# Tail of an attention and SwiGLU kernel in rounds of four products and four output steps

## The chip, the cores and the metric

The kernel runs on one core of a Trainium2 chip. The metric is the device time of one execution in microseconds (us). Before the change the median of three runs was 777.21 us (777.11, 777.21 and 779.03).

## The reference, cut to what matters

Eight batches of 512 tokens with 256 channels pass one transformer block and a conditioned layer norm, all in 32-bit floats:

```python
x = x + a_alpha * attention(ada_rmsnorm(x, t, attn_gamma_w, attn_beta_w), W_q, W_k, W_v, W_o)   # 16 heads of 16
h = ada_rmsnorm(x, t, ffn_gamma_w, ffn_beta_w)
x = x + f_alpha * (silu(h @ gate_w.T) * (h @ hidden_w.T) @ out_w.T + out_b)                     # hidden width 1024
out = (layernorm(x) * weight + bias + tanh(t @ lin_w.T + lin_b)) * weight + bias
```

`gamma`, `beta` and `alpha` are one row per batch, made from the 64 numbers of `t`. Every projection is made as a sum of three products of high and low parts, so one 256-wide contraction of a tile takes six matmuls or, in tiles of 64 rows, twelve.

## The kernel before, in words

Each engine has its own instruction stream, written by a Python function `unit(n)` that is called for n = 0, 1, 2, ... up to `LAST` = 164. Semaphores tie the streams together. There are 16 units per batch. For n below `NU` = 128 a unit does one 128-key block of attention for one group of four heads. From n = `GH_AT` = 28 on, each unit also has one **product** of the feed-forward part, number e = n - 28, from 0 to 127.

- **Product e** (`gate_hidden`, L1323): 24 matmuls in tiles of 64 rows, two side by side, for hidden columns 128 (e mod 8) and on, of half batch e // 8 (256 tokens). The gate and the value land in two banks of PSUM. Then ScalarE takes the tanh (L861), VectorE makes the silu and multiplies (L1070, L1077, `act_y`), ScalarE rounds to the high part (L868, `a_hi`), and the low part `a_lo` is made by GpSimd (L554) while attention runs, by VectorE (L1083) in the tail. `a_hi` and `a_lo` are rings of six.
- **Output step e** (`project_out`, L1336): 6 matmuls with the full 128 rows that add product e's share to the output of the half. It waits for `a_lo` of e.
- **Jobs** are other pieces of TensorE work given to units by a table. In the tail four are left, all of the last batch (7): `WO` 0 and 1 (projection of the attention output, L1210, units 134 and 135), `FT` 0 and `FT` 1 (transposes of the normalised half, L1248, units 137 and 141), which make the inputs of products 112 to 119 and 120 to 127.

The **tail** begins at n = 128, where the scores of the last attention block are done. TensorE has products 100 to 127, output steps 96 to 127, the last `attend` (L1296) and the four jobs left. `tail_units` writes them in rounds. Three pairs of banks (`ps_m`, `ps_x`, `ps_s`) take the products in turn, so product e waits for `act_y` of product e - 3. All output steps of a half add up in the bank `ps_o`; when eight are done VectorE multiplies the sum by `f_alpha` (`scale(("H", half))`, L1042), GpSimd adds it to x (`add_to_x`, L579), VectorE takes mean and variance (`statistics`, L1062) and GpSimd normalises (`moments`, `normalise`, `weigh`). The first output step of the next half waits for that multiplication.

Before `WO` 0 of batch 7 can run, the output of the last attention group goes a long way: ScalarE copies it out of PSUM (L845), it is written to memory, the sums of the softmax are read back, inverted, written and broadcast (`out_scratch`, `d_s`, `reciprocal_scratch`, `d_c`), GpSimd multiplies (L562), ScalarE rounds (L854) and GpSimd makes the low part (L567, `on_lo`). Before product 112 can run, `WO` 0 is scaled and added to x, squared on ScalarE (L742), the root taken on GpSimd (L510, L512), normalised (L771), transposed (`FT` 0), split in high and low parts (L825, L996, L1004), and a DMA swaps the two halves of the rows (`n_x`, L378); the second half of the product's matmuls reads `n_x`. The same goes for `FT` 1 and product 120.

The order of each stream is the order in which the functions are called; a wait on one instruction holds all that is behind it on that engine.

Of the kernel before, what the change touches and what calls it, by code (L numbers as in the profile page):

```python
# [12 lines left out]
B = 8  # L13
# [10 lines left out]
JC = HID // P  # L24
# [3 lines left out]
UNITS = NG * TT  # L28
NU = B * UNITS
# [6 lines left out]
GH_AT = 28  # L36
# [35 lines left out]
def chunk_at(n):  # L72
# [3 lines left out]


SC = sorted([(CHUNK_AT + CH * c, 0, ("F", c)) for c in range(CHUNKS)]
            + [(GH_AT + LAG + JC * (hf + 1), 0, ("H", hf)) for hf in range(CHUNKS * CH // JC, 2 * B)]
            + [(n, 1, job_at(n)) for n in range(LAST) if job_at(n) and job_at(n)[0] == "WO"])  # L80
SC_NO = {what: no + 1 for no, (_, _, what) in enumerate(SC)}

# [6 lines left out]
def build(nc, dram):  # L89
    with ExitStack() as ctx:  # L90
# [401 lines left out]
        def _(pool):  # L492
# [76 lines left out]
            def add_to_x(what):  # L569

                hf = {"F": what[1] * CH // JC, "H": what[1]}.get(what[0])
                b, h = (what[2], what[1]) if what[0] == "WO" else (hf // 2, hf % 2)
                pool.wait_ge(sc_r, SC_NO[what])
                if what[0] == "WO":
                    pool.wait_ge(xr_in[h][b % 2], 16 * (b // 2 + 1))
                else:
                    pool.wait_ge(bias_r, 2 * b + h + 1)
                xs = xr[:, b % 2, 2 * h:2 * h + 2]
                pool.tensor_tensor(xs, xs, sc[:], ALU.add).then_inc(x_add, 1)  # L579
# [77 lines left out]
            def unit(n):  # L657
                b, u = n // UNITS, n % UNITS
                e = n - GH_AT - 1

                def at(k, d):
                    return u == k and 0 <= b + d < B

                if at(0, 1):
                    n_low(b + 1, 0)
                if at(1, 1):
                    n_low(b + 1, 1)
                if job_at(n - 1) and job_at(n - 1)[:2] == ("FT", 1) and n < NU:
                    n2_low(job_at(n - 1)[2], 1)
                if at(4, -1):  # L670
                    o_norm(b - 1, 1)
                if at(10, -1) and n < NU:
                    n2_low(b - 1, 0)
                if at(11, -2):
                    moments(b - 2, 0)
                    normalise(b - 2, 0)
                if at(10, 2):
                    root1(b + 2)
                if at(12, -1) and n < NU:
                    norm2(b - 1, 1)  # L680
                if at(13, 0):
                    o_norm(b, 0)
                if chunk_at(n - 1) is not None:
                    add_to_x(("F", chunk_at(n - 1)))
                if 0 <= e < TAIL:
                    a_low(e)
                if n in PIECE_AT:
                    split_piece(PIECE_AT.index(n))
                if at(1, -3) and b - 3 < B - 1:
                    moments(b - 3, 1)  # L690
                    normalise(b - 3, 1)
                    weigh(b - 3, 1)
                if at(1, 0) and b > 0:
                    v_copy(b, 3)
                if at(5, -1):
                    o_low(b - 1, 1)
                if at(6, -2) and n >= NU:
                    add_to_x(("H", 2 * (b - 2)))
                if at(7, -1) and n < NU:
                    add_to_x(("WO", 0, b - 1))  # L700
                if at(8, -1) and n < NU:
                    norm2(b - 1, 0)
                    add_to_x(("WO", 1, b - 1))
                if n == NU + 7:
                    root2(B - 1, 0)
                if n == NU + 9:
                    root2(B - 1, 1)
                if at(9, -1):
                    add_bias(b - 1, 0)
                if at(11, -2):  # L710
                    weigh(b - 2, 0)
                if at(13, -1):
                    add_bias(b - 1, 1)
                if at(14, 1):
                    for g in range(NG - 1):
                        v_copy(b + 1, g)
                if at(14, 0):
                    o_low(b, 0)
                if at(14, -2) and NU <= n < LAST - JC:
                    add_to_x(("H", 2 * (b - 2) + 1))  # L720

            for n in range(LAST):
                unit(n)
# [248 lines left out]
        def _(dve):  # L972
# [59 lines left out]
            def scale(what):  # L1032

                no = SC_NO[what]
                if no > 1:
                    dve.wait_ge(x_add, no - 1)
                if what[0] in "FH":
                    step = {"F": CH, "H": JC}[what[0]]
                    end = step * (what[1] + 1)
                    dve.wait_ge(f_done, end)  # L1040
                    dve.wait_ge(tab_f_in, 16 * ((end - 1) // (2 * JC) + 1))
                    dve.tensor_tensor(sc[:], ps_c if what[0] == "F" else ps_f, tab_f[:].unsqueeze(1).broadcast_to([P, 2, D]),  # L1042
                                      ALU.mult).then_inc(sc_r, 1)
                else:
                    dve.wait_ge(job_full, JOB_NO[what])
                    dve.wait_ge(tab_a_in, 16 * (what[2] + 1))
                    dve.tensor_tensor(sc[:], ps_j[:].rearrange("p (t n) -> p t n", t=2),
                                      tab_a[:, 0:1, :].broadcast_to([P, 2, D]), ALU.mult).then_inc(sc_r, 1)
# [37 lines left out]
            def last_norm():  # L1086

                hf = 2 * B - 1
                dve.wait_ge(sc_r, SC_NO["H", hf])
                dve.wait_ge(bias_r, hf + 1)  # L1090
                xs = xr[:, hf // 2 % 2, 2:4]
                dve.tensor_tensor(xs, xs, sc[:], ALU.add).then_inc(x_add, 1)
                statistics(B - 1, 1)
                dve.wait_ge(mv_r, 2 * (hf + 1))
                for t in range(2):
                    dve.scalar_tensor_tensor(out=xs[:, t], in0=xs[:, t], scalar=mv[:, t, 0:1], in1=w2[:],
                                             op0=ALU.subtract, op1=ALU.mult).then_inc(z_last_r, 1)
                dve.wait_ge(rstd3_r, hf + 1)
                for t in range(2):
                    dve.wait_ge(z_last_r, t + 1)  # L1100
                    dve.scalar_tensor_tensor(out=xs[:, t], in0=xs[:, t], scalar=rstd3[:, t:t + 1], in1=tab_b[:],
                                             op0=ALU.mult, op1=ALU.add).then_inc(z_last_r, 1)
# [39 lines left out]
            def unit(n):  # L1142
                b, u = n // UNITS, n % UNITS
                e = n - GH_AT

                def at(k, d):
                    return u == k and 0 <= b + d < B

                if n == 0:
                    evac(("TR", 0, 1), n)  # L1150
                if n + LEAD < NU:
                    reduce_max(2 * (n + LEAD))
                if n + LEAD < NU:
                    reduce_max(2 * (n + LEAD) + 1)
                if at(6, -2) and n >= NU:
                    scale(("H", 2 * (b - 2)))
                if at(14, -2) and n >= NU:
                    scale(("H", 2 * (b - 2) + 1))
                if 0 <= e < TAIL:
                    gate(e)  # L1160
                if at(10, -2):
                    statistics(b - 2, 0)
                if at(0, -3) and b - 3 < B - 1:
                    statistics(b - 3, 1)
                if chunk_at(n) is not None:
                    scale(("F", chunk_at(n)))
                if job_at(n) and n < NU:
                    evac(job_at(n), n)
                if at(2, -1):
                    o_recip(b - 1, 1)  # L1170
                if at(11, 0):
                    o_recip(b, 0)
                if TAIL <= e - 1 < NE:
                    a_low(e - 1)
                if TAIL <= e < NE:
                    gate(e)
                if job_at(n) and n >= NU:
                    evac(job_at(n), n)
# [6 lines left out]
        def _(pe):  # L1185
# [267 lines left out]

            def tail_units(n):
                e = n - GH_AT
                for d in range(2):
                    if e + d < NE:
                        gate_hidden(e + d)
                if n == NU:
                    attend(n - 1)  # L1460
                job(n)
                for d in range(CHUNKS * CH if n == NU else e - 2, e):
                    if d < NE:
                        project_tail(d)
                job(n + 1)

            for n in range(GH_AT):
                early_unit(n)
            for n in range(GH_AT, NU):
                middle_unit(n)  # L1470
            for n in range(NU, LAST, 2):
                tail_units(n)

# [27 lines left out]
```

## Time and profile before

| | |
|---|---|
| median of three runs | 777.21 us |
| the profiled execution, its own time | 781.7 us |
| its span, first to last instruction | 779.9 us |
| mean granted clock of TensorE | 0.976 of full |
| busy: TensorE, VectorE, ScalarE, GpSimd | 721.0, 536.2, 470.8, 392.1 us |

The busy share of TensorE is 92% of the span, and in most of the 40 slices of the page it is 90% or more. The tail lies in the last four slices, from about 694 us on. The granted clock is 1.00 in most stretches and lower in a few: 1.00 stands for 2.4 GHz, 0.50 for 1.2 GHz. Matmuls are pipelined, so a matmul that lasts 0.28 us can be followed by the next one 0.12 us after its start; what a piece of work costs is read from the distance of starts, or from the chain of waits.

### The profile page before, as it was taken

How to read it: one execution, taken by the hardware profiler on the slowest of the kernel's cores; microseconds unless marked ns; L12 is line 12 of the kernel's file. 1: busy time of each engine (PE TensorE's matmuls, PEld its weight loads, DVE VectorE, ACT ScalarE, POOL GpSimd, SP SyncE). 2: the span in 40 equal slices, each digit the busy share in tenths (PEclk: the TensorE clock that was granted, in tenths of full speed). 3: DMA queues.
4: the chain of work that ended last, by engine and by line, in shares of the span. 5: the costliest groups of instructions: out<-in, count | busy, mean ns of one | idle time of the engine just before them, and what ended most of it. 6: DMA issues, size and time to landing. Idle time of an engine off the chain costs nothing.

```text
span 779.9 us, 17477 instructions
## 1 busy us (share of the span) xinstructions
PE 721.0 (92%) x6646; PEld 489.3 (63%) x6646; DVE 536.2 (69%) x795; ACT 470.8 (60%) x858; POOL 392.1 (50%) x493
## 2 busy tenths in 40 slices
PE   5678787899999999999999999999999999999995
PEld 4333233455676767675676667776677667679895
DVE  3576675678667776777667776768667776536765
ACT  4347574778566756667666756667666655753431
POOL 4335331345248553666348553766447453872433
PEclk9769998999999999999999999999999999999998
DMA  6855655445442644445442553445443440242110
GB/s 193 270 176 182 203 189 166 163 124 210 132 165 68 202 144 148 140 137 183 132 164 80 192 162 131 137 137 158 137 157 102 172 141 15 58 116 64 49 50 28
DMA packets 63676, 108.75 MB, mean 139 GB/s; under 512 B 10240, under 2 KB 17848, under 8 KB 63592
## 3 DMA queue, kind: packets, MB, share of 16 engines
q1 hardware_dynamic: 62760, 106.78, 43.0%
q8 instruction: 53, 0.87, 0.5%
q10 hardware_dynamic: 704, 0.66, 0.3%
q0 software_dynamic: 128, 0.20, 0.1%
q14 instruction: 31, 0.25, 0.1%
HBM read 59.60 MB, written 39.09 MB: 127 GB/s over the span
## 4 chain that ended last, share of the span: by engine, by line
PE 69%; DVE 9%; DMA 8%; issue 6%; ACT 4%; SPq 3%; POOL 1%; ACTq 0%; POOLq 0%; DVEq 0%
PE ps_x L1323 16%; PE ps_j L1210 11%; PE ps_o L1296 11%; PE ps_j L1336 9%; PE ps_s L1283 9%; PE ps_m L1270 6%; DVE mx L1030 4%; DMA out_scratch<-o_raw 2%; PE ps_o L1336 2%; ACT prob L837 2%; DVE fx L996 2%; DMA qs<-m_hl 1%; DVE gate_t L1070 1%; PE ps_m L1323 1%; DMA prob<-in_wk 1%
## 5 line engine op out<-in xcount | busy, mean ns | idle before, releaser
L1030 DVE TENSOR_REDUCE mx<-ps_m 128x2 f32<-128x1024 f32 x222 | 271.6, 1223 | 126.4 <-PE ps_m L1270 125.9
L837 ACT ACTIVATE prob<-ps_s 128x1024 f32<-128x1024 f32 x256 | 262.0, 1024 | 82.4 <-PE ps_s L1283 81.8
L1283 PE MATMUL ps_s<-qs,ks 64*128 64x512 f32 x512 | 120.4, 466 | 21.5 <-ACT prob L837 15.0
L1296 PE MATMUL ps_o<-prob,v 128*32 128x512 f32 x1024 | 139.0, 615 | 0.2 <-ACT o_raw L845 0.2
L1283 PEld LDWEIGHTS ps_s<-qs,ks 64*128 64x128 f32 x512 | 48.7, 186 | 141.0 <-issue 73.8
L1270 PE MATMUL ps_m<-ks,qs 64*128 64x512 f32 x444 | 94.0, 419 | 9.3 <-DVE mx L1030 5.6
L1323 PE MATMUL ps_x<-n,gh_hi 64*128 64x256 f32 x872 | 97.8, 284 | 1.6 <-DVE act_y L1077 1.6
L554 POOL TENSOR_TENSOR a_lo<-act_y,a_hi 128x256 fp32r<-128x256 f32 x100 | 73.7, 737 | 46.5 <-ACT a_hi L868 46.3
L1323 PE MATMUL ps_x<-n_x,gh_hi 64*128 64x256 f32 x872 | 94.3, 276 | 0.0
L579 POOL TENSOR_TENSOR xr<-xr,sc 128x512 f32<-128x512 f32 x41 | 53.3, 1300 | 63.1 <-DVE sc L1042 40.6
L1323 PEld LDWEIGHTS ps_x<-n,gh_hi 64*128 64x128 f32 x872 | 74.3, 184 | 13.6 <-DVE act_y L1077 10.1
L1323 PEld LDWEIGHTS ps_x<-n_x,gh_hi 64*128 64x128 f32 x872 | 74.4, 185 | 0.0
L868 ACT ACTIVATE a_hi<-act_y 128x256 fp32r<-128x256 f32 x128 | 52.7, 412 | 27.2 <-DVE act_y L1077 27.2
L562 POOL TENSOR_TENSOR d_c<-on_lo,d_c 128x512 f32<-128x512 f32 x16 | 20.6, 1287 | 92.0 <-DMA d_c<-reciprocal_scratch 92.0
L861 ACT ACTIVATE gate_t<-ps_x 128x256 f32<-128x256 f32 x109 | 41.8, 383 | 34.6 <-PE ps_x L1323 34.1
L1323 PE MATMUL ps_x<-n,gh_lo 64*128 64x256 f32 x436 | 61.1, 276 | 0.0
L1323 PE MATMUL ps_x<-n_x,gh_lo 64*128 64x256 f32 x436 | 61.1, 276 | 0.0
L1336 PE MATMUL ps_j<-ow_hi,a_hi 128*128 128x256 f32 x192 | 56.5, 294 | 0.0
L1270 PEld LDWEIGHTS ps_m<-ks,qs 64*128 64x128 f32 x444 | 43.1, 190 | 20.1 <-DVE mx L1030 15.6
L1070 DVE SCALAR_TENSOR_TENSOR gate_t<-gate_t,ps_x 128x256 f32<-128x256 f32 x109 | 44.8, 411 | 13.8 <-ACT gate_t L861 13.8
L1336 PE MATMUL ps_j<-ow_hi,a_lo 128*128 128x256 f32 x192 | 54.0, 281 | 0.0
L1336 PE MATMUL ps_j<-ow_lo,a_hi 128*128 128x256 f32 x192 | 54.0, 281 | 0.0
(176 smaller groups left out, 1439.6 us busy)
## 6 DMA issues: line engine op xcount, KB each, us to landing
qs<-stack_scratch SPq DMA_DIRECT2D x31, 512.0 KB, 5.1
ks<-stack_scratch SPq DMA_DIRECT2D x31, 512.0 KB, 6.4
stack_scratch<-qk_hi SPq DMA_DIRECT2D x56, 256.0 KB, 3.2
out_scratch<-o_raw SPq DMA_DIRECT2D x32, 256.0 KB, 2.9
n_x<-n SPq DMA_DIRECT2D x32, 256.0 KB, 3.7
stack_scratch<-qk_lo SPq DMA_DIRECT2D x28, 256.0 KB, 3.5
on_lo<-out_scratch SPq DMA_DIRECT2D x16, 256.0 KB
d_c<-reciprocal_scratch SPq DMA_DIRECT2D x16, 256.0 KB
```

The lines of the kernel that those rows point to most:

```text
L554: pool.tensor_tensor(a_lo[:, e % RING, :], act_y[:, e % 2, :], a_hi[:, e % RING, :].bitcast(F32), ALU.subtract)\
L579: pool.tensor_tensor(xs, xs, sc[:], ALU.add).then_inc(x_add, 1)
L837: act.activation(prob[:, n % 2, 2 * h:2 * h + 2, :], ps_s[:], ACT.Exp, scale=SCALE).then_inc(p_r, 1)
L868: act.activation(a_hi[:, e % RING, :], act_y[:, e % 2, :], ACT.Copy).then_inc(a_hi_r, 1)
L1030: dve.tensor_reduce(mx[:, group % 2, :, h, qt], max_pair(mp)[:], AX.X, ALU.max).then_inc(mx_red, 1)
L1070: dve.scalar_tensor_tensor(out=gate_t[:], in0=gate_t[:], scalar=1.0, in1=g_part(e), op0=ALU.add, op1=ALU.mult).then_inc(s_r, 1)
L1210: mm = pe.matmul(out, lhs(a, k), rhs(c, k), start=(n == 0), stop=(n == len(steps) - 1))
L1270: mm = pe.matmul(max_pair(mp)[:, s, :], qs[r:r + 64, g, j, qt * P:(qt + 1) * P], ks[r:r + 64, g, j, :], start=True, stop=True)
L1283: mm = pe.matmul(ps_s[:, s, :], ks[r:r + 64, g, j, kb * P:(kb + 1) * P], qs[r:r + 64, g, j, :], start=True, stop=True)
L1296: mm = pe.matmul(ps_o[32 * i:32 * i + 32, :], v[:, g, kb, i, :], prob[:, n % 2, i, :], start=(kb == 0), stop=(kb == TT - 1), skip_group_ch ...
L1323: mm = pe.matmul(bank[:, r, 0:HT], GH[a][rows, 2 * k + (r ^ x), j * P:(j + 1) * P], N2[x][rows, h, c, k, :], start=(m == 0), stop=(m == 11))
L1336: mm = pe.matmul(out[:, t, :], A[a][:, e % RING, t * P:(t + 1) * P], OW[c][:, j, :], start=(first and m == 0 and t == 0), stop=(end and m ...
```

## The change

`tail_units` writes four products, then up to three jobs, then four output steps, then a fourth job, where it wrote two products, a job, two output steps and a job. The last `attend` keeps its place behind product 101. The other streams keep one unit per product. Because a half's last output step now stands at another place in TensorE's stream, the units at which VectorE and GpSimd take up the sum of a half are moved: for halves 12 to 14 from n = 134, 142 and 150 to n = 136, 144 and 152, which puts the sum of half 12 behind `WO` 0 and `WO` 1. Statistics and normalisation of half 13 go two units later (n = 144 to 146, 145 to 147). The scaling of half 15 moves from the stream's unit 158 into `last_norm`.

```diff
-            + [(GH_AT + LAG + JC * (hf + 1), 0, ("H", hf)) for hf in range(CHUNKS * CH // JC, 2 * B)]
+            + [(NU + (GH_AT + JC * (hf + 1) - NU + 3) // 4 * 4 + 4, 0, ("H", hf)) for hf in range(CHUNKS * CH // JC, 2 * B)]
 # GpSimd
-                if at(1, -3) and b - 3 < B - 1:
+                if at(1 if n < NU + UNITS else 3, -3) and b - 3 < B - 1:
                     moments(b - 3, 1)
-                if at(6, -2) and n >= NU:
+                if at(8, -2) and n >= NU:
                     add_to_x(("H", 2 * (b - 2)))
-                if at(14, -2) and NU <= n < LAST - JC:
-                    add_to_x(("H", 2 * (b - 2) + 1))
+                if at(0, -3) and NU < n < LAST - JC:
+                    add_to_x(("H", 2 * (b - 3) + 1))
 # VectorE
             def last_norm():
                 hf = 2 * B - 1
+                scale(("H", hf))
-                if at(6, -2) and n >= NU:
+                if at(8, -2) and n >= NU:
                     scale(("H", 2 * (b - 2)))
-                if at(14, -2) and n >= NU:
-                    scale(("H", 2 * (b - 2) + 1))
+                if at(0, -3) and NU < n < LAST - JC:
+                    scale(("H", 2 * (b - 3) + 1))
-                if at(0, -3) and b - 3 < B - 1:
+                if at(0 if n < NU + UNITS else 2, -3) and b - 3 < B - 1:
                     statistics(b - 3, 1)
 # TensorE
             def tail_units(n):
                 e = n - GH_AT
-                for d in range(2):
+                for d in range(4):
                     if e + d < NE:
                         gate_hidden(e + d)
-                if n == NU:
-                    attend(n - 1)
-                job(n)
-                for d in range(CHUNKS * CH if n == NU else e - 2, e):
+                    if n + d == NU + 1:
+                        attend(NU - 1)
+                for d in range(3):
+                    job(n + d)
+                for d in range(e - 4, e):
                     if d < NE:
                         project_tail(d)
-                job(n + 1)
+                job(n + 3)
-            for n in range(NU, LAST, 2):
+            for n in range(NU, LAST, 4):
                 tail_units(n)
```

The order that this gives on TensorE in the whole tail, in short (P product, O output step, A the last attend):

```
before: P100 P101 A O96-99 | P102 P103 O100 O101 | P104 P105 O102 O103 | P106 P107 WO0 O104 O105 WO1 |
        P108 P109 O106 O107 FT0 | P110 P111 O108 O109 | P112 P113 O110 O111 FT1 | ... | P126 P127 O124 O125 | O126 O127
after:  P100 P101 A P102 P103 O96-99 | P104-107 WO0 O100-103 WO1 | P108-111 FT0 O104-107 |
        P112-115 FT1 O108-111 | P116-119 O112-115 | P120-123 O116-119 | P124-127 O120-123 | O124-127
```

TensorE at the last attend (first row), before the change:

```order
L1296 MATMUL ps_o<-prob,v 32x512 x4
L1336 MATMUL ps_o<-ow_hi,a_hi 128x256
L1336 MATMUL ps_o<-ow_hi,a_lo 128x256
L1336 MATMUL ps_o<-ow_lo,a_hi 128x256
L1336 MATMUL ps_o<-ow_hi,a_hi 128x256
```

and with it:

```order
L1297 MATMUL ps_o<-prob,v 32x512 x4
L1324 MATMUL ps_s<-n,gh_hi 128x256 x2
L1324 MATMUL ps_s<-n,gh_lo 128x256 x2
L1324 MATMUL ps_s<-n,gh_hi 128x256 x4
L1324 MATMUL ps_s<-n,gh_lo 128x256 x2
```

Product 102 now stands where output step 96 stood; the four output steps follow behind product 103.

TensorE at `FT` 0 of batch 7 (the row with `fx`), before:

```order
L1336 MATMUL ps_o<-ow_hi,a_hi 128x256
L1336 MATMUL ps_o<-ow_hi,a_lo 128x256
L1336 MATMUL ps_o<-ow_lo,a_hi 128x256
L1248 MATMUL ps_j<-ident,fx 128x128 x4
L1323 MATMUL ps_x<-n,gh_hi 128x256 x2
L1323 MATMUL ps_x<-n,gh_lo 128x256 x2
```

and with the change:

```order
L1324 MATMUL ps_s<-n_x,gh_lo 128x256 x2
L1324 MATMUL ps_s<-n_x,gh_hi 128x256 x2
L1249 MATMUL ps_j<-ident,fx 128x128 x4
L1337 MATMUL ps_o<-ow_hi,a_hi 128x256
L1337 MATMUL ps_o<-ow_hi,a_lo 128x256
L1337 MATMUL ps_o<-ow_lo,a_hi 128x256
```

`FT` 0 stood between output step 107 and product 110; it now stands between product 111 and output step 104.

VectorE around the two `WO` jobs (L1047, L1013) and the sum of half 12 (L1042), where the rows with a minus are of before and those with a plus of after:

```order
+L1047 TENSOR_TENSOR sc<-ps_j,tab_a 128x512
+L1013 TENSOR_TENSOR xr<-xr,sc 128x512
 L1042 TENSOR_TENSOR sc<-ps_o,tab_f 128x512
 L1083 TENSOR_TENSOR a_lo<-act_y,a_hi 128x256
-L1070 SCALAR_TENSOR_TENSOR gate_t<-gate_t,ps_m 128x256
-L1077 TENSOR_TENSOR act_y<-ps_m,gate_t 128x256
-L1047 TENSOR_TENSOR sc<-ps_j,tab_a 128x512
-L1013 TENSOR_TENSOR xr<-xr,sc 128x512
```

The sum of half 12 is taken up behind both `WO` jobs and no longer ahead of them. No stream has an instruction more or less than before; those of ScalarE and of the DMA queue keep their order.

## Rows read from the trace of the kernel before

**Rows 1.** Waits of TensorE in the tail, 694.4 to 772 us.

```profile
PE ps_o L1336 <- DVE a_lo L1083: 2.5, 2, 1.5
PE ps_j L1210 <- POOL on_lo L567: 0.7, 1, 0.7
PE ps_o L1336 <- ACT o_raw L845: 0.7, 1, 0.7
PE ps_m L1323 <- DMA n_x<-n: 0.4, 1, 0.4
PE ps_o L1336 <- DVE sc L1042: 0.4, 1, 0.4
```

**Rows 2.** Chain of waits, last attend to WO 0: start us, us, what.

```profile
697.57 1.04 PE ps_o L1296 x8
...
699.25 2.03 DMA out_scratch<-o_raw
...
708.10 3.64 DMA d_c<-reciprocal_scratch
...
713.90 1.29 POOL on_lo L567
...
715.33 1.67 PE ps_j L1210 x12
```

**Rows 3.** Chain of waits: output steps in pairs (x12), products one by one (x24).

```profile
717.00 1.42 PE ps_o L1336 x12
...
744.62 1.61 PE ps_o L1336 x12
746.23 1.60 PE ps_m L1323 x24
747.83 1.40 PE ps_x L1323 x24
```

**Rows 4.** Timeline of VectorE: start us, us, line, tiles; silu part of product 100.

```profile
699.99 0.42 DVE L1077 TENSOR_TENSOR act_y<-ps_m,gate_t 128x256 f32<-128x256 f32 x1
```

**Rows 5.** Chain of waits, FT 0 to the second half of product 112.

```profile
724.45 0.45 PE ps_j L1248 x4
...
728.54 3.52 DMA n_x<-n
...
732.11 0.97 PE ps_m L1323 x12
```

**Rows 6.** Timeline at the end of the tail; brackets: idle before, and releaser.

```profile
769.86 1.26 POOL L638 TENSOR_TENSOR xr<-xr,tab_b 128x512 f32<-128x512 f32 x1
769.90 1.50 DVE L1083 TENSOR_TENSOR a_lo<-act_y,a_hi 128x256 fp32r<-128x256 f32 x1 [0.48 <-ACT a_hi L868]
```

**Rows 7.** Chain of waits, the last output step.

```profile
771.46 0.99 PE ps_o L1336 x6
```

**Rows 8.** Timeline of TensorE: gaps by waits on a DMA.

```profile
28.79 0.79 PE L1270 MATMUL ps_m<-ks,qs 64*128 64x512 f32 x2 [2.21 <-DMA ks<-stack_scratch]
...
93.71 0.79 PE L1283 MATMUL ps_s<-qs,ks 64*128 64x512 f32 x2 [2.96 <-DMA qs<-m_hl]
...
128.03 0.80 PE L1283 MATMUL ps_s<-qs,ks 64*128 64x512 f32 x2 [3.11 <-DMA qs<-m_hl]
```

**Rows 9.** TensorE by microsecond: stretch, its length, busy, PEclk, DMA share, GB/s.

```profile
93.00:94.00 1.00, 0.29 (x2) 0.64 0.13 22
...
96.00:97.00 1.00, 1.00 (x6) 0.65 0.93 236
...
127.00:128.00 1.00, 0.00 (x0) 0.71 0.10 22
...
134.00:135.00 1.00, 1.00 (x8) 0.88 0.87 338
```

**Rows 10.** Timeline of TensorE at half clock: first and sixth of six equal matmuls.

```profile
132.79 0.41 PE L1210 MATMUL ps_j<-w_lo,n_hi 128*128 128x256 f32 x1
...
133.85 0.41 PE L1210 MATMUL ps_j<-w_hi,n_lo 128*128 128x256 f32 x1
```

## The prediction, made before the changed kernel ran

> **What bounds the kernel now.** First I read the page: TensorE is busy for 92% of the span, so what the change is worth depends on whether TensorE in the tail still has something to do at every moment. Next the waits of TensorE between 694.4 and 772 us [rows 1]: four kinds, together 4.7 us of idle time, the largest 1.5 us just ahead of the last output step. So the tail is bound by TensorE's own work, with a few short waits. Then the chain of waits, for two stretches that TensorE does not set: the way of the attention output into `WO` 0 [rows 2], and the way of `FT` 0 into product 112 [rows 5]. Last the clock by microseconds, where TensorE waited long [rows 8, 9].
>
> **Prices.** A product costs 1.40 us behind another product and 1.60 behind a tile of another shape; two output steps cost 1.42 us behind work in full tiles and 1.61 behind a product [rows 3]. Each change of shape thus costs 0.20 us, a single output step 0.71 us. The six low-clock matmuls of the same size stand 1.06 / 5 = 0.212 us apart [rows 10]; at full clock it is 1.42 / 12 = 0.118 us [rows 3]. So a microsecond of TensorE work done at half clock loses 1 - 0.118 / 0.212 = 0.44 us.
>
> **What is removed.** From 28 changes of shape in the tail 15 are left (there are half as many rounds, but product 102 now stands behind attend). 13 x 0.20 = 2.6 us less. The wait of output step 96 for `o_raw` (0.7) goes, since products 102 and 103 stand in front of it. The wait at the end (1.5) goes too: there the last `a_lo` lasted 1.50 us, beside a GpSimd pass of 1.26 us [rows 6], and only three output steps stood between product 127 and the last step; now seven do, 5 us, and `a_lo` of 127 is due some 4 us behind product 127. I give `a_lo` the same 1.5 us; without that cover the 1.5 us would be back.
>
> **What is added, first gap.** `WO` 0 starts at 715.33 [rows 2], 16.7 us behind the end of attend at 698.61, after three transfers and two GpSimd passes. None of these waits for TensorE, and attend keeps its place, so `WO` 0 cannot start sooner with the change. What TensorE has ahead of it shrinks by output steps 100 to 103. By hand: product 102 from 698.5 to 700.1; product 103 takes the banks of product 100 and waits for its `act_y`, over at 699.99 + 0.42 = 700.41 [rows 4], so it runs from 700.5 to 701.9; steps 96 to 99 take 1.61 + 1.42, to 704.9; products 104 to 107 take 1.60 + 3 x 1.40 = 5.8, to 710.8. Their banks are free in time: tanh, silu, high part and low part of a product are some 2.2 us together, and one product starts every 1.4 us with three pairs of banks. From 710.8 to 715.3 TensorE has nothing: **4.5 us of idle time**, where 0.7 stood.
>
> **Second gap.** From 715.33: `WO` 0 1.67, steps 100 to 103 2.84, `WO` 1 1.42, products 108 to 111 1.60 + 4.20, and `FT` 0 begins at 727.06 on the chain's reckoning, 0.2 later still as its shape differs from the product in front of it. Before it stood at 724.45, and from there to the second half of product 112 the chain took 732.11 - 724.45 = 7.66 us, of which 3.52 is the swap `n_x` [rows 5]. That way is ScalarE, VectorE and DMA, all unchanged, so `n_x` is there at 727.26 + 7.66 = 734.9. ScalarE has the normalised half ready about 724, so `FT` 0 waits for nothing but its turn. The cover behind `FT` 0 is itself, 0.65, steps 104 to 107, 2.84, and the first half of product 112, 0.90: to 731.45. **Idle for 3.5 us**, where 0.4 stood. Before, two products and two steps (4.4 us) lay there. On GpSimd `root2` of the first half now stands ahead of the sum of half 12, a pass of 1.3 us, but ScalarE's squares do not come earlier (they stand behind tanh 107, which waits for step 100), so I cost that at nothing.
>
> **The rest.** From 734.9: second half of product 112 0.97, products 113 to 115 4.20, `FT` 1 0.65, steps 108 to 111 2.84; twice four products and four steps, 5.80 + 3.03 each; then products 124 to 127 5.80 and eight steps 1.61 + 4.26. Together 38.0 us, plus 0.3 for a wait of product 119 for `act_y` of 116, which is held up by the statistics of half 13. That ends at 773.2; before it ended at 771.46 + 0.99 = 772.45 [rows 7]. Behind it VectorE scales and normalises half 15 as before. So at full clock the change costs **+0.8 us**: the idle time added takes all that the shapes and the short waits give back. The sums of halves 13 and 14, their statistics and normalisation end 10 us or so before somebody needs them; two units later they are hidden by products.
>
> **The clock.** Every gap of TensorE of 2.2 us or more in the middle of its work was followed by half clock: 2.21, 2.96 and 3.11 us [rows 8]. From the clock means, the second one fell at 93.28 (0.64 is 0.28 at full and 0.72 at half) and rose at 96.70, which is 3.0 us of work at 1.2 GHz behind the gap's end at 93.71; the third fell at 127.42 and rose at 134.24, 6.2 us behind 128.03 [rows 9]. Both new gaps, 4.5 and 3.5 us, are longer than these. So a fall costs 3.0 x 0.44 = 1.3 to 6.2 x 0.44 = 2.7 us; the two rows are equally near, I take 4.6 us and 2.0 us for each gap. All of it is on the path, as behind both gaps TensorE has work without a wait. The Trainium skill ("TensorE: Matmul & The Clock Gate", "Why this matters for your kernels") says that long idle gaps between bursts of matmuls bring the half clock back; by that rule, which speaks against this change, the loss is there as in the rows; without it the sum would stay at +0.8.
>
> **Sum.** +0.8 + 2 x 2.0 = +4.8 us. The profiled execution took 781.7 us (span 779.9) against a median of 777.2; the difference does not touch a change in the tail, so I add to the median: **782.0 us**. Bounds of the unknown: both falls at the low row +3.4 (780.6), both at the high row +6.2 (783.4).
>
> The 0.20 us per change of shape has a rival price on the page "TensorE: Matmul & The Clock Gate" of the Trainium skill ("LDWEIGHTS"): 128 columns at 1.2 GHz, 0.107 us, if just one weight load were laid bare; 13 changes would then give an estimate of 1.4 us instead of 2.6, and the sum would be 1.2 us higher. The trace's own 0.20 decides.
>
> **Rivals.**
> - *One fall only.* The second gap is broken by half a product, and the clock may stay up, or the second fall may overlap less work. +0.8 + 1.3 to 2.7: 779.3 to 780.7. Against it: 2.21 us sufficed once.
> - *No fall.* 778.0, no change that can be told. For it: I have three gaps only, all in attention, none among work in full tiles.
> - *Faster.* The attention output reaches `WO` 0 sooner than it did: three transfers lie in that chain, and `out_scratch` took 2.03 us where the page's median to landing is 2.9, so they vary. If they took 3 us less, the old order could have gained 0.7 of it and the new one gains all: 2.3 better than +0.8, the first gap shrinks to 1.5 us and does not lower the clock. With the second gap's clock kept as well: 777.2 + 0.8 - 2.3 = 775.7. It decides once the chain is shorter by 1.5 us or more. Against it: this transfer was quick already.
> - *Worse.* Transfers longer by 1 us each widen both gaps: +3 on the high row, 785.
>
> **How the numbers follow.** Chances: both falls 0.62, one fall 0.18, none 0.09, faster 0.05, worse 0.06. A measurement of this kernel tells a change from none at about 0.3%, 2.3 us. Slower by more: 0.62 + 0.06 + 0.11 of the one-fall case = 0.79; within: 0.09 + 0.07 = 0.16; faster 0.05. The range runs from 778.6, which leaves out no fall and the faster case, to 784.0.
>
> **What would show it.** In the new trace: `WO` 0 at the same distance from attend, with 4 to 5 us of idle time on TensorE ahead of it; product 112 waiting 3 to 4 us for `n_x`; granted clock of 0.50 behind both; no wait ahead of the last output step; 1.61 us for the first pair of steps of a round and 1.42 for the second. The forecast is wrong if the clock stays at 1.00 behind the gaps, or if `WO` 0 starts well before 16.7 us behind attend.

## The result and the profile after

With the change the kernel takes 782.81 us (median of seven runs, 779.23 to 784.36) against 779.03 us before (seven runs, 776.51 to 780.95, the first three included); the ratio is 1.0048 with a 95% interval of 1.0027 to 1.0069, which is 3.7 us, 2.1 to 5.4. It is slower, by half a percent. The profiled execution has a span of 782.5 us.

A whole run varies by some us with what happens in its first 170 us: attend ends at 698.61 us in the trace of before and at 695.92 in the trace of after, though both run the same instructions up to there. (In all twelve traces the attention part from about 170 to about 690 us takes the same time to 0.3 us.) So below the traces are compared by two stretches of the chain of waits: the **tail**, from the end of the last attend to the end of the last output step, and the **late tail**, from the start of `WO` 0 to the same end. The tail took 73.84 us before [rows 2, 7] and 775.08 - 695.92 = 79.16 after; the late tail 57.12 and 62.16.

The waits of TensorE in the tail of after (us in total, times, longest), which answer to [rows 1]:

```profile
PE ps_j L1211 <- POOL on_lo L567: 4.6, 1, 4.6
PE ps_m L1324 <- DMA n_x<-n: 3.3, 1, 3.3
PE ps_m L1324 <- DVE act_y L1077: 0.3, 1, 0.3
```

The six short waits of before have become two long ones and one short one. `o_raw`, the sum of half 13 and the two `a_lo` no longer hold anything up; `on_lo` and `n_x` hold up six and eight times as much.

The chain of waits of after, answering to [rows 2, 3, 5, 7] (start us, us, what):

```profile
694.88 1.04 PE ps_o L1297 x8
...
712.92 2.90 PE ps_j L1211 x12
715.82 3.09 PE ps_o L1337 x24
...
726.12 0.60 PE ps_j L1249 x4
...
730.36 3.52 DMA n_x<-n
...
733.93 1.65 PE ps_m L1324 x12
735.58 2.56 PE ps_x L1324 x24
738.14 2.37 PE ps_s L1324 x24
...
760.37 3.03 PE ps_o L1337 x24
...
769.20 5.88 PE ps_o L1337 x48
```

`WO` 0 starts 17.0 us behind attend (16.7 before). Its twelve matmuls take 2.90 us, not 1.67, and the products behind `n_x` take 2.56 and 2.37 us, not 1.40: that is half clock. Four output steps cost 3.03 us, one change of shape for four; the last eight run through without a wait. The granted clock by microseconds (stretch, length, busy, PEclk, DMA share, GB/s), answering to [rows 9]:

```profile
712.00:713.00 1.00, 0.08 (x1) 0.93 0.00 0
713.00:714.00 1.00, 1.00 (x5) 0.50 0.08 16
...
716.00:717.00 1.00, 1.00 (x10) 0.87 0.00 0
...
733.00:734.00 1.00, 0.07 (x2) 0.67 0.01 4
...
740.00:741.00 1.00, 1.00 (x20) 0.92 0.00 0
```

From 712.86 to 716.26 and from 733.34 to 740.16 TensorE had 1.2 GHz: 3.3 and 6.2 us of work behind the ends of the gaps at 712.92 and 733.93.

### The profile page after: what moved, and what is told of

Same layout as the page of the kernel before. It is cut to its first block, busy times and chain, and to the rows that moved or that the text cites. A ratio compares the mean times of both kernels' runs of the same rounds, so it can differ in the third digit from the quotient of the medians.

```text
span 782.5 us, 17477 instructions
## 1 busy us (share of the span) xinstructions
PE 720.2 (92%) x6646; PEld 491.3 (63%) x6646; DVE 535.3 (68%) x795; ACT 469.6 (60%) x858; POOL 391.8 (50%) x493
## 4 chain that ended last, share of the span: by engine, by line
PE 68%; DMA 10%; DVE 9%; issue 5%; ACT 4%; SPq 3%; POOL 1%; ACTq 0%; POOLq 0%; DVEq 0%
PE ps_x L1324 16%; PE ps_j L1211 11%; PE ps_o L1297 11%; PE ps_j L1337 9%; PE ps_s L1284 8%; PE ps_m L1271 6%; DVE mx L1030 3%; DMA out_scratch<-o_raw 3%; PE ps_o L1337 2%; ACT prob L837 2%; DMA qs<-m_hl 2%; DVE fx L996 2%; PE ps_m L1324 1%; PE ps_s L1324 1%; DVE gate_t L1070 1%
## 5 line engine op out<-in xcount | busy, mean ns | idle before, releaser
L1284 PEld LDWEIGHTS ps_s<-qs,ks 64*128 64x128 f32 x512 | 48.5, 185 | 140.5 <-issue 71.3
L1324 PEld LDWEIGHTS ps_x<-n,gh_hi 64*128 64x128 f32 x872 | 74.9, 186 | 13.3 <-DVE act_y L1077 10.0
L1070 DVE SCALAR_TENSOR_TENSOR gate_t<-gate_t,ps_x 128x256 f32<-128x256 f32 x109 | 44.8, 411 | 11.8 <-ACT gate_t L861 11.7
```

The source lines that it names most:

```text
L1070: dve.scalar_tensor_tensor(out=gate_t[:], in0=gate_t[:], scalar=1.0, in1=g_part(e), op0=ALU.add, op1=ALU.mult).then_inc(s_r, 1)
L1284: mm = pe.matmul(ps_s[:, s, :], ks[r:r + 64, g, j, kb * P:(kb + 1) * P], qs[r:r + 64, g, j, :], start=True, stop=True)
L1324: mm = pe.matmul(bank[:, r, 0:HT], GH[a][rows, 2 * k + (r ^ x), j * P:(j + 1) * P], N2[x][rows, h, c, k, :], start=(m == 0), stop=(m == 11))
```

## The experiments

The granted clock and the chain of each kernel come from one trace per kernel; the ratios come from 7 to 12 timed runs of each (e5, e8 and e10 have the profiled run alone). Each kernel's late tail is read from its trace by the same two rows of the chain, the start of `WO` 0 and the last output steps:

| kernel | WO 0 starts | last step ends | late tail | against before | ratio to before (95%) |
|---|---|---|---|---|---|
| before | 715.33 | 772.45 | 57.12 | | |
| the change | 712.92 | 775.08 | 62.16 | +5.04 | 1.0048 (1.0027 to 1.0069) |
| e1 both gaps filled | 713.07 | 770.99 | 57.92 | +0.80 | 1.0002 (0.9983 to 1.0021) |
| e5 first gap filled | 709.77 | 769.23 | 59.46 | +2.34 | one run |
| e8 second gap filled | 717.04 | 776.40 | 59.36 | +2.24 | one run |
| e10 first gap in part, second filled | 711.72 | 769.58 | 57.86 | +0.74 | one run |
| e2 FT 0 sooner | 715.69 | 772.58 | 56.89 | -0.23 | 1.0008 (0.9987 to 1.0029) |
| e6 steps 100 to 103 ahead of WO 0 | 711.42 | 769.16 | 57.74 | +0.62 | 1.0022 (1.0003 to 1.0041) |
| e3 fours from unit 144 on | 709.04 | 763.24 | 54.20 | -2.92 | 0.9967 (0.9941 to 0.9993) |
| e4 fours from unit 136, FT 0 sooner | 714.25 | 767.87 | 53.62 | -3.50 | 0.9953 (0.9931 to 0.9975) |
| e7 as e4, step 108 sooner | 710.07 | 763.71 | 53.64 | -3.48 | 0.9944 (0.9923 to 0.9964) |
| e9 as e7, FT 1 sooner | 717.74 | 770.65 | 52.91 | -4.21 | 0.9918 (0.9892 to 0.9944) |

### e1: both gaps filled

```diff
+            def keep_busy(count):
+                job_evacuated(last[0])
+                for _ in range(count):
+                    pe.matmul(ps_j[:, 0:D], ow_hi[:, 0, 0:P], ow_lo[:, 0, :], start=True, stop=True)
 # in gate_hidden
+                if e == 112:
+                    keep_busy(24)
 # in job, ahead of run
+                    if job_at(n) == ("WO", 0, B - 1):
+                        keep_busy(34)
```

Expected:

> The changed kernel with matmuls whose result nobody reads in both gaps of TensorE: 34 ahead of WO 0 (34 x 0.118 = 4.0 of the 4.6 us) and 24 ahead of product 112 (2.8 of the 3.3 us). My theory (gaps set by chains that do not touch TensorE, plus half clock behind each): WO 0 and n_x come no sooner, the granted clock stays at 1.00 behind both, and the 9.5 us of work at 1.2 GHz give back 9.5 x 0.44 = 4.2 us; ratio to before 1.001 (+0.8 to +1.1 us). Rival, that the clock is not the cause and the rounds of four cost by themselves: ratio stays at 1.005.

Waits of TensorE in this kernel:

```profile
PE ps_j L1211 <- POOL on_lo L567: 0.6, 1, 0.6
PE ps_m L1332 <- DMA n_x<-n: 0.4, 1, 0.4
```

and its chain at both ends of the late tail:

```profile
713.07 1.69 PE ps_j L1211 x12
714.76 2.84 PE ps_o L1345 x24
...
765.11 5.88 PE ps_o L1345 x48
```

`WO` 0 came 17.3 us behind attend, no sooner than in the others, so the filling took nothing away from the chain; its matmuls took 1.69 us and the steps behind it 2.84, full clock. The clock stayed at 1.00 from attend to the last output step. The late tail is 0.80 us longer than before, the full-clock term of the prediction; 4.2 us of the 5.0 belong to the clock. The time agrees (1.0002, interval 0.9983 to 1.0021).

### e5, e8 and e10: one gap at a time, and a short gap

The same edit with `keep_busy(34)` alone (e5), `keep_busy(24)` alone (e8), and with 22 and 24 (e10).

Expected of e5:

> The changed kernel with only the first gap filled (34 matmuls whose result nobody reads, ahead of WO 0). Measured by the tail, from the end of the last attend to the end of the last output step: 73.84 us before, 79.16 with the change, 75.18 with both gaps filled. My theory, each gap with its own stretch at half clock: the granted clock stays at 1.00 behind WO 0 and still falls behind the wait for n_x, which stays 3.3 us; the tail is shorter by the 3.3 us at 1.2 GHz x 0.44 = 1.5 us: 77.7 us (plus or minus 0.5 for the transfers). Rival, one fall brings the other: the second stretch goes too and the tail is 75 us.

Expected of e8:

> The changed kernel with only the second gap filled (24 matmuls whose result nobody reads, ahead of product 112). My theory: the clock falls behind the first gap and stays at 1.00 behind the second; the stretch of 6.2 us at 1.2 GHz, 2.7 us, is given back: tail 79.2 - 2.7 = 76.5 us; the first stretch may last 3.0 to 6.2 us, which makes it 76.3 to 77.8. Rival, that the long stretch behind the second gap comes from the shape of the work there and not from the idle time: the clock falls all the same and the tail stays at 79 us.

Expected of e10:

> The changed kernel with 22 matmuls whose result nobody reads ahead of WO 0 (2.6 of the 4.6 us, so that 2.0 us of idle time are left) and 24 ahead of product 112. Gaps of 1.7 us so far left the clock up, one of 2.2 us and all longer ones were followed by half clock. If the length of the gap decides between these, 2.0 us is open: with no fall the stretch from WO 0 to the end of the last step is 57.9 us as with both gaps filled, with a fall of 3.3 us at 1.2 GHz 59.4 us.

In e5 the clock stayed up behind `WO` 0 and fell behind `n_x`; in e8 the other way round, behind a wait of 4.7 us. So neither fall brings the other (one trace of each). The tail of e5 is 769.23 - 692.73 = 76.5 us, less than the 77.7 expected, since the second stretch at 1.2 GHz was shorter here. Waits and granted clock of e5:

```profile
PE ps_m L1330 <- DMA n_x<-n: 3.3, 1, 3.3
PE ps_j L1211 <- POOL on_lo L567: 0.4, 1, 0.4
```

```profile
729.00:730.00 1.00, 0.69 (x10) 1.00 0.00 0
730.00:731.00 1.00, 1.00 (x18) 0.68 0.08 16
...
733.00:734.00 1.00, 1.00 (x14) 0.62 0.66 260
```

The clock was down from 730.36 to 733.76, 3.4 us.

e8 has a tail of 776.40 - 700.03 = 76.4 us (76.5 expected); its stretch behind `WO` 0 also lasted 3.4 us. The same 3.3 us gap thus cost 2.7 us in the trace of after and 1.5 in e5: what varies from run to run is the length of the stretch.

In e10 the wait for `on_lo` was 1.6 us by the trace and the clock stayed at 1.00 all through the tail; the late tail is that of e1. 2.0 us had been expected to remain, so the length that was to be tried was not reached: `WO` 0 came 16.7 us behind attend here and 17.0 in the trace of after, and the 22 matmuls pushed the gap's start back by 2.8 us and not 2.6.

In the tails of the twelve traces, then, the six gaps of 3.3 us or more were each followed by a fall, those up to 1.7 us (e4, e6, e7, e10) by none, and up to the last output step no fall came without such a gap. The attention part of the same traces shows that length alone does not decide, and that the expectation's "all longer ones" goes too far. The first pair of rows is from the trace of after, the second from e10, the third again from after (for each the timeline of TensorE, then the clock):

```profile
93.00 0.51 PE L1284 MATMUL ps_s<-qs,ks 64*128 64x512 f32 x2 [3.05 <-DMA qs<-m_hl]
93.00:94.00 1.00, 1.00 (x8) 1.00 0.00 0
```

```profile
124.03 0.50 PE L1284 MATMUL ps_s<-qs,ks 64*128 64x512 f32 x2 [1.75 <-DMA qs<-m_hl]
...
125.00:126.00 1.00, 1.00 (x8) 0.50 0.23 27
```

```profile
139.02 0.50 PE L1284 MATMUL ps_s<-qs,ks 64*128 64x512 f32 x2 [0.67 <-ACT prob L837]
139.00:140.00 1.00, 0.98 (x8) 0.71 0.34 121
```

A gap of 3.05 us left the clock at 1.00, one of 1.75 us was followed by a fall, and about 139.4 us the clock fell with no gap over 0.9 us in the 5 us before. From gaps between 1.75 and 3.05 us both outcomes are on record. What else decides is not shown.

### e2: FT 0 two products sooner

```diff
                 for d in range(4):
                     if e + d < NE:
                         gate_hidden(e + d)
 # two lines left out: the last attend
+                    if job_at(n + d) == ("FT", 0, B - 1):
+                        job(n + d)
                 for d in range(3):
-                    job(n + d)
+                    if job_at(n + d) != ("FT", 0, B - 1):
+                        job(n + d)
```

Expected:

> The changed kernel with FT 0 of batch 7 behind product 109 instead of behind product 111; all else equal. My theory: FT 0 starts 2.8 us sooner, products 110 and 111 come to lie beside the way to n_x, the wait of product 112 falls from 3.3 to 0.5 us or less and the second stretch at half clock (6.2 us, 2.7 us lost) goes; two more changes of shape cost 0.4: about 5.5 us less than the changed kernel, ratio to before 0.999 to 1.000. Rival, that ScalarE's normalised half is not ready by then: FT 0 waits instead, the gap moves ahead of product 110 and the time stays near ratio 1.004.

```profile
PE ps_j L1211 <- POOL on_lo L567: 4.7, 1, 4.7
PE ps_m L1324 <- DMA n_x<-n: 0.6, 1, 0.6
```

The late tail fell by 5.3 us against the change (5.5 expected). `FT` 0 did not wait, the wait for `n_x` went from 3.3 to 0.6 us and the second stretch at half clock is gone; the first is still there. The way of `n_x` itself was no shorter, so the second gap is a matter of how much work TensorE has between `FT` 0 and product 112. The time agrees within its interval (1.0008, 0.9987 to 1.0029).

### e6: output steps 100 to 103 ahead of WO 0

```diff
                 for d in range(3):
-                    job(n + d)
+                    if n + d != NU + 6:
+                        job(n + d)
                 for d in range(e - 4, e):
                     if d < NE:
                         project_tail(d)
+                if n + 2 == NU + 6:
+                    job(n + 2)
                 job(n + 3)
```

Expected:

> The changed kernel with output steps 100 to 103 ahead of WO 0, which is followed at once by WO 1. My theory: the first gap falls from 4.6 to 1.7 us, too short for a fall of the clock (1.5 back); WO 1 now waits some 0.9 us for the scaling of WO 0; together WO 1 ends 1.9 us sooner; the second gap and its fall stay: tail 79.2 - 1.9 - 1.5 = 75.8 us, ratio to before 1.002. Rival, that the first gap is not what holds the tail but the way from WO 0 to FT 0: the second gap grows by what the first loses, tail 77.5 us or more.

```profile
PE ps_m L1324 <- DMA n_x<-n: 3.4, 1, 3.4
PE ps_j L1211 <- POOL on_lo L567: 1.7, 1, 1.7
PE ps_j L1211 <- DVE sc L1047: 0.8, 1, 0.8
```

The three waits are nearly as expected (1.7, 0.8 for 0.9, and an unchanged second gap), the clock stayed up behind the gap of 1.7 us, and the ratio is as expected too (1.0022 for 1.002). The tail is 769.16 - 694.30 = 74.9 us, 0.9 less than 75.8: again a second stretch of 3.4 and not 6.2 us. The rival, by which the second gap would grow, is out.

### e3 and e4: where rounds of four pay

e3 starts from the kernel before and gives `tail_units` a size, 2 for n up to 142 and 4 from 144 on, takes the output steps up where the round before left off, and moves the sum of half 14 alone to unit 152. Of the edit, the calls alone:

```diff
-            for n in range(NU, LAST, 2):
-                tail_units(n)
+            for n in range(NU, NU + 16, 2):
+                tail_units(n, 2)
+            for n in range(NU + 16, LAST, 4):
+                tail_units(n, 4)
```

Expected:

> Rounds of two as before up to unit 142, rounds of four from unit 144 on (products 116 to 127); the sum of half 14 two units later. My theory: neither gap opens; six changes of shape fewer (1.2 us) and no wait ahead of the last output step (1.5 us), 0.3 us lost to one wait for act_y: 2.4 us faster than before, ratio 0.997. Rival, that a change of shape costs nothing and only shows in the records: ratio 0.998 by the last wait alone; rival, that rounds of four stall on the banks: 1.000 or more.

```profile
741.12 1.61 PE ps_o L1336 x12
...
748.53 3.03 PE ps_o L1336 x24
757.36 5.88 PE ps_o L1336 x48
```

The last eight output steps run without a wait; the waits for `on_lo`, `n_x`, the first `a_lo` and the sum of half 13 are there as before. The late tail is 2.92 us shorter, half a microsecond more than expected (the wait for `act_y` that was to cost 0.3 did not come), and the ratio is 0.9967: faster, by a third of a percent. The last wait alone would give 1.5 us, so the changes of shape have their price; the interval of the time (0.9941 to 0.9993) cannot tell 0.998 from 0.997, the late tail from end to end can.

e4 has the two sizes meet at unit 136 and `FT` 0 behind product 109 as in e2.

Expected:

> Rounds of two up to unit 134 (so WO 0 and WO 1 stand as before), rounds of four from unit 136 with FT 0 behind product 109; sum of half 12 at unit 134, of 13 and 14 as in the changed kernel. My theory: WO 0 waits 0.7 us as before, n_x is there about 730.6 on the clock of the first trace and product 112 waits 1.5 us for it, too short for a fall of the clock; then 38.0 us of work: 3 to 3.6 us faster than before, ratio 0.9955 to 0.996. Rival, that a wait of 1.5 us already lowers the clock: 0.998 to 1.000.

```profile
PE ps_m L1324 <- DMA n_x<-n: 1.7, 1, 1.7
PE ps_j L1211 <- POOL on_lo L567: 0.2, 1, 0.2
```

3.50 us shorter, ratio 0.9953. The wait for `n_x` is 1.7 us for 1.5 expected, and the clock stayed up behind it.

### e7: one output step into the wait for n_x, a miss

```diff
-                for d in range(next_step[0], min(e, NE)):
+                end = 109 if n == NU + 8 else min(e, NE)
+                for d in range(next_step[0], end):
                     project_tail(d)
-                next_step[0] = e
+                next_step[0] = end
```

Expected:

> The mixed kernel with output step 108 (and 106, 107) ahead of product 112. Its step stood behind product 115. My theory: the 1.7 us wait of product 112 for n_x is filled by one step, 0.71 us, all else stays: tail 69.78 - 0.7 = 69.1 us, ratio to before 0.9945. Rival, that a_lo of 108 is late on VectorE, behind FT 0's work there: the step waits, product 112 starts later than n_x lands, and the tail stays at 69.8 or grows.

```profile
PE ps_j L1211 <- POOL on_lo L567: 1.6, 1, 1.6
PE ps_m L1324 <- DMA n_x<-n: 1.0, 1, 1.0
PE ps_s L1324 <- DVE act_y L1077: 0.2, 1, 0.2
```

The step did fill 0.7 us of the wait, and the late tail stayed at 53.64 us. (The ratio came out as 0.9944 for 0.9945 expected, but its interval and that of e4 overlap, so it does not tell the two kernels apart. The tail as a whole is 71.3 us, since `WO` 0 came 17.6 us behind attend here and 16.2 in e4: the transfers.) Not `a_lo`, the rival, took it back, but the work of `FT` 1. From the chain of e7:

```profile
730.56 0.60 PE ps_j L1249 x4
...
732.24 0.99 DVE fx L996 x2
...
734.61 0.44 DVE act_y L1077
...
735.09 1.66 PE ps_s L1324 x24
736.78 1.69 PE ps_m L1324 x24
738.50 1.68 PE ps_x L1324 x24
```

and from the chain of e4:

```profile
734.74 0.60 PE ps_j L1249 x4
...
742.67 1.67 PE ps_x L1324 x24
```

ScalarE and VectorE have `FT` 1's parts to make behind product 113, and TensorE reaches `FT` 1 behind product 115; VectorE comes to the silu of product 114 only then. The rows at 735.09, 736.78 and 738.50 are products 117, 118 and 119: each waits for the `act_y` of the product three before, and they start 1.7 us apart where 1.40 is the price. The list of waits shows only 0.2 us of this, since it counts from the modelled end of a matmul. From `FT` 1 to product 119 both kernels take 7.9 us (730.56 to 738.50 and 734.74 to 742.67): in e4 TensorE's own work just filled that way, and what the step took out of the wait for `n_x` was waited off here.

### e9: FT 1 sooner as well

```diff
             def early(n):
-                return job_at(n) == ("FT", 0, B - 1)
+                return job_at(n) in (("FT", 0, B - 1), ("FT", 1, B - 1))
```

Expected:

> The kernel of e7 with FT 1 of batch 7 behind product 113 instead of behind product 115. From the start of WO 0 to the end of the last output step e7 took 53.64 us and the mixed kernel 53.62, though its wait for n_x was 0.7 us shorter. My theory of that: ScalarE and VectorE come to FT 1's work behind product 113 and stand still until TensorE reaches it behind product 115, so act_y of product 113 is late and product 116 waits for its banks; what the step saved was waited off there. With FT 1 sooner that wait (0.7 us or more) goes and two changes of shape (0.4) come in: 53.0 to 53.3 us, ratio to before 0.994. Rival, that output steps 108 to 111 are themselves held up (by a_lo): the stretch stays at 53.6 or grows by 0.4.

```profile
717.74 1.66 PE ps_j L1211 x12
...
764.77 5.88 PE ps_o L1337 x48
```

52.91 us, 0.73 less than e7, though it has two changes of shape more: the wait for `act_y` is gone from the trace. (The products that waited in e7 were 117 to 119, behind the silu of 114 to 116, and not 116 as the expectation has it; the cause that it names, VectorE and ScalarE standing still until `FT` 1, is what the trace shows.) This is the shortest late tail of all, 4.2 us under before. Of 780 us that would be a ratio of 0.9946; the timed 0.9918 is lower, with an interval (0.9892 to 0.9944) that just leaves 0.9946 out; why it is lower is not shown.

## Why the prediction was right, point by point

- **The time.** 782.0 us forecast, 782.8 measured; but the median of before rose by 1.8 us with more runs, so that the two agree to 0.8 us is in part luck and the difference is what counts: +4.8 us forecast, +3.7 (2.1 to 5.4) measured, +5.3 in the tail of the profiled execution.
- **The waits of before.** The rows hold five kinds, six waits, and not four kinds; the sum of 4.7 us is right.
- **First gap.** 4.5 us of idle time forecast, 4.6 found; `WO` 0 at 16.7 us behind attend forecast, 17.0 found, and 16.2 to 17.6 over all the traces, whatever TensorE did in front of it (e1, e5 and e10 filled the gap and e6 put other work there). The way holds four transfers (`out_scratch`, `d_s`, `reciprocal_scratch`, `d_c`), not three; nothing in the sum hangs on their number.
- **Second gap.** 3.5 forecast, 3.3 found. e2 shows the cause.
- **Full-clock term.** +0.8 forecast; e1 has +0.80 in the late tail, where the tail alone would say +1.3, as the chain to `WO` 0 was half a microsecond longer in that run. Its parts agree too: `WO` 0 to `FT` 0 11.7 us (11.9 forecast), `FT` 0 to the second half of product 112 7.8 (7.7), from there to the end 38.4 (38.3).
- **The 0.3 us of product 119.** It was found, but the statistics of half 13 do not cause it: they come after. The chain of e1 and of after leads from `FT` 1 over VectorE's work for it and the sum of half 13 to product 119, 7.9 us, as in e4 and e7.
- **What was removed.** Last wait, `o_raw` wait and cheaper rounds are all there: 3.03 us for four output steps where twice 1.61 stood. e3 shows the last wait and the shapes together in time.
- **The clock, a term somewhat too large.** Two falls, as forecast. I took 4.6 us of work at half clock for each, from two rows of 3.0 and 6.2. The trace of after has just these, 3.3 and 6.2. But in e2, e5, e6 and e8 each stretch at 1.2 GHz lasted 3.4 us, five of the six in all, so the usual loss is 1.5 us per gap: 0.8 + 2 x 1.5 = 3.8 us. The 3.7 of the timed runs fits this, but their interval, 2.1 to 5.4, holds the 4.8 as well.
- **The falls, right with some luck.** "Every gap of 2.2 us or more" was three gaps of one trace. The trace of after has a gap of 3.05 us in attention with no fall, e3 one of 2.2 us. That both new gaps lowered the clock fits the forecast and its 0.62; that gaps of this length always do was never shown, though all six in the tails did.
- **The rivals.** "One fall only" and "no fall" did not happen in the profiled execution of the change; e2 and e6 each had one long gap left, and one fall. "Faster" asked for a chain to `WO` 0 shorter by 1.5 us or more; none of the traces had that. "Worse" has a slip in its sum: +3 on the high row would be 786.4, not 785. The rival price of a change of shape, 1.4 us for all 13, is refuted in its size by the 3.03 and 1.61 us rows: 3.03 - 4 x 0.71 is 0.19. Its mechanism is not: a weight load of an output step lasts 0.19 us in the trace of before, so one load laid bare would cost just that. No run tells whether it is the load.

Not settled: what besides its length decides whether a gap is followed by half clock, why a stretch at half clock is at times twice as long, and what share of the timed runs has it.

## What to carry to other kernels

Fewer switches between kinds of work are worth what the rows say (here 0.2 us each), but the work that is moved was also the cover of something: before regrouping, write down for every outside chain (transfers, another engine) how much TensorE work lies beside it in the old and in the new order. If a gap opens that is as long as gaps that the traces show to be followed by half clock, add that price, times the share of such gaps that were; look at every such gap in several traces, since one trace had only three. Here the price of two falls was about four times the rest. And regroup only where no chain needs the cover: fours behind unit 136, with the transposes pulled forward, turned 3.7 us of loss into some 4 us of gain (e9).

## What was not expected of the hardware

The clock can fall after the work has begun again. In e5 product 112 went on at 729.3 and the clock fell at 730.36 (rows above). In e6 the gap ended at 729.3 as well, and the clock fell at 730.84:

```profile
730.00:731.00 1.00, 1.00 (x22) 0.92 0.00 0
...
734.00:735.00 1.00, 1.00 (x18) 0.88 0.07 16
```

In both it was back 3.4 us after the fall. So a gap whose end still shows 1.00 may still be paid for, a microsecond or so into the work behind it.

The same transfers and passes between attend and `WO` 0 took from 16.2 us (e4) to 17.6 us (e7), though e4 and e7 have the same instructions there. That is more than the effect of several of the edits, and the reason why the late tail is the better measure here.
